# Totals of the cross-attention softmax with queries on the partitions

## The reference

```python
q = (x @ Wq).reshape(B, N, 16, 32).transpose(0, 2, 1, 3)        # 16 heads of 32, N = 224 queries
k = (context @ Wk).reshape(B, M, 16, 32).transpose(0, 2, 1, 3)  # M = 750 keys
v = (context @ Wv).reshape(B, M, 16, 32).transpose(0, 2, 1, 3)
attn = softmax(where(mask, q @ k.T * scale, max_neg), axis=-1)
out = (attn @ v).transpose(0, 2, 1, 3).reshape(B, N, 512) @ Wo
```

## Time and profile before

| | us |
|---|---|
| median of 3 runs | 4072.93 (4070.74 to 4074.32) |
| the profiled execution | 4072.49 |
| its span, from the first to the last instruction | 4070.7 |
| PE busy, whole span | 3752.8 (92%) |
| DVE busy | 2371.8 (58%) |
| ACT busy | 1741.6 (43%) |
| POOL busy | 1300.7 (32%) |

### The profile page before, as it was taken

One profiled execution on the slowest core, in us unless ns is written; L12 is line 12 of the kernel. 1 busy time (PEld: TensorE's weight loads), 2 busy tenths in 40 slices (PEclk: granted clock), 3 DMA queues, 4 the chain that ended last, 5 costly groups with the idle time before them and its releaser, 6 DMA issues. The chain is left out here.

```text
span 4070.7 us, 85297 instructions
## 1 busy us (share of the span) xinstructions
PE 3752.8 (92%) x28101; PEld 3217.9 (79%) x28101; DVE 2371.8 (58%) x5513; ACT 1741.6 (43%) x4280; POOL 1300.7 (32%) x1200
## 2 busy tenths in 40 slices
PE   6999999999679999999999998638999999999997
PEld 5888888888567887778877775637898898988986
DVE  4888888888546665666656664573434433334342
ACT  3545545555335555555555553103333333333332
POOL 1333333333225555555555554001102012022011
PEclk8999999999889999999999998558999999999998
DMA  3122222222233433334333431504333243233231
GB/s 110 50 61 60 56 56 65 52 61 52 91 97 99 108 101 95 103 103 107 101 96 102 103 90 49 148 6 112 94 98 111 76 117 111 80 109 111 85 99 53
DMA packets 319070, 354.23 MB, mean 87 GB/s; under 512 B 45135, under 2 KB 231991, under 8 KB 318996
## 3 DMA queue, kind: packets, MB, share of 16 engines
q1 hardware_dynamic: 309396, 325.67, 29.6%
q0 software_dynamic: 9600, 27.58, 2.4%
HBM read 189.05 MB, written 38.65 MB: 56 GB/s over the span
## 5 line engine op out<-in xcount | busy, mean ns | idle before, releaser
L1482 DVE TENSOR_REDUCE x_mx<-x_psS 112x1 f32<-112x752 f32 x512 | 481.4, 940 | 454.5 <-PE x_psS L1092 450.4
L2200 DVE TENSOR_TENSOR hid<-e_psU,act_g 128x280 f32<-128x280 f32 x256 | 115.1, 450 | 759.1 <-PE e_psU L34 759.1
L1330 ACT ACTIVATE x_pt<-x_psE 125x448 f32<-125x448 f32 x768 | 389.5, 542 | 324.5 <-PE x_psE L1104 318.7
L1004 POOL TENSOR_TENSOR part<-x_pt 125x448 f32<-125x448 f32 x256 | 292.5, 1142 | 608.7 <-ACT x_pt L1330 608.4
L2028 POOL TENSOR_TENSOR ex_y<-ex_y,ex_cur 112x2560 f32<-112x2560 f32 x8 | 45.5, 5691 | 1041.2 <-ACT ex_y L2176 1041.2
L562 POOL TENSOR_TENSOR qks<-qks,cos 128x448 f32<-128x448 f32 x128 | 147.8, 1154 | 699.1 <-DMA qks<-qk 699.1
L1092 PE MATMUL x_psS<-k_st,q_st 97*112 97x376 f32 x1024 | 284.7, 359 | 37.5 <-DVE x_mx L1482 22.9
L2133 ACT ACTIVATE act_g<-e_psG 128x280 f32<-128x280 f32 x256 | 103.6, 405 | 497.6 <-PE e_psG L34 497.5
L32 PE MATMUL e_psG<-ex_hi,g_hi 128*128 128x280 f32 x1024 | 299.6, 293 | 8.0 <-DVE g_lo L2194 6.7
L32 PE MATMUL pj<-xT_hi,win_hi 128*128 128x224 f32 x1024 | 303.1, 296 | 1.8 <-DVE xT_lo L634 1.7
L34 PE MATMUL e_psG<-ex_hi,g_lo 128*128 128x280 f32 x1024 | 298.9, 292 | 0.0
(11 more groups left out here) (280 smaller groups left out, 10847.8 us busy)
## 6 DMA issues: line engine op xcount, KB each, us to landing
k_st<-kT SPq DMA_DIRECT2D x768, 93.8 KB, 2.1
raw_g<-in_L_ffn_wg SPq DMA_DIRECT2D x128, 256.0 KB, 3.2
raw_u<-in_L_ffn_wu SPq DMA_DIRECT2D x128, 256.0 KB, 3.4
raw_d<-in_L_ffn_wd SPq DMA_DIRECT2D x128, 256.0 KB, 2.7
qks<-qk SPq DMA_DIRECT2D x512, 56.0 KB, 2.0
q_st<-qT SPq DMA_DIRECT2D x384, 56.0 KB, 2.0
ctxt<-in_ctx SPq DMA_DIRECT2D x16, 1125.0 KB
xt<-in_x SPq DMA_DIRECT2D x16, 448.0 KB, 3.6
```

Of the source, the lines that this page charges most:

```text
L1004: pool.tensor_tensor(part[:], pt[j][:, 0, :], pt[j][:, 1, :], ALU.add).then_inc(parted, 1)
L1330: act.activation(pt[j][:, i, :], psE[(j + i) % 2][0:KR, 0:2 * T], ACT.Exp, scale=XD ** -0.5).then_inc(exp_done, 1)
L1482: dve.tensor_reduce(mx[:, j, h:h + 1], psS[0:HT, :, 0:376], AX.XY, ALU.max).then_inc(s_taken, 1)
L2200: dve.tensor_tensor(h[i][:, halves[s]], psU[:, 0:CH], act_g[i][:, halves[s]], ALU.mult).then_inc(S["mul"], 1)
```

## The change

The totals are made the other way round. ptsum of a head, 112 queries at a time, becomes the weights, and one column of ones is streamed: 8 products give psTot, 112 queries on the partitions x 8 columns (half h, head j). One reciprocal over 112x8 inverts them. A copy on DVE spreads each column to 32 columns (rzb, 112 x 2 x 128). PE turns both halves back with two transposes into psZ (turn_totals), ACT copies psZ to SBUF (out_totals, rzT, 128x224), and out_y multiplies psY by that. turn_totals stands behind scores (2, 1) on PE; out_totals behind the last exponential of head 2 on ACT; invert is one call, behind maximum (2, 0).

```diff
-            yT, rz = sb(c, "x_yT", [P, KD, T]), sb(c, "x_rz", [P, T])
+            yT, rz, rzb = sb(c, "x_yT", [P, KD, T]), sb(c, "x_rz", [HT, 8]), sb(c, "x_rzb", [HT, 2, P])
+            rzT = sb(c, "x_rzT", [P, T])
...
-            psY, psZ = psYZ[:, 0:T], psYZ[:, T:2 * T]
+            psY, psZ, psTot = psYZ[:, 0:T], psYZ[:, T:2 * T], psYZ[0:HT, 2 * T:2 * T + 8]
...
                         pe.wait_ge(pt_summed, 4 * t + 4)
                         for j in range(4):
-                            m = pe.matmul(psZ[32 * j:32 * j + 32, 0:T], ones[:], ptsum[4 * (g % 2) + j][:], start=True, stop=True)
+                            for h in range(2):
+                                m = pe.matmul(psTot[:, 4 * h + j:4 * h + j + 1], ptsum[4 * (g % 2) + j][:, h * HT:(h + 1) * HT], ones[:, 0:1],
+                                              start=True, stop=True)
                         m.then_inc(z_full, 1)
+
+                    def turn_totals(t):
+
+                        pe.wait_ge(z_spread, t + 1)
+                        for h in range(2):
+                            m = pe.transpose(psZ[:, h * HT:(h + 1) * HT], rzb[:, h, :], ident[0:HT, 0:HT])
+                        m.then_inc(z_turned, 1)
...
                             scores(n, g, 2, 1)
+                            if pprev:
+                                turn_totals(n - 2)
...
                     shifted(n - 1, 3, 3, range(3))
+                    turn_totals(n - 2)
                     values(n - 1, 3)
                     totals(n - 1, 3)
+                    turn_totals(n - 1)
...
+                    def out_totals(t):
+                        act.wait_ge(z_turned, t + 1)
+                        act.activation(rzT[:], psZ, ACT.Copy).then_inc(z_out, 1)
...
                                 exps(n - 1, 2, (2,))
+                            if not (first and g < 2):
+                                out_totals(n - 2)
...
                     for j in range(1, 4):
                         exps(n - 1, j, range(3))
+                    for k in (2, 1):
+                        out_totals(n - k)
...
-                    def invert(t, i):
+                    def invert(t):
 
                         dve.wait_ge(z_full, t + 1)
-                        cols = slice(i * HT, i * HT + HT)
-                        dve.reciprocal(rz[:, cols], psZ[:, cols]).then_inc(recip, 1)
+                        dve.reciprocal(rz[:], psTot).then_inc(recip, 1)
+                        dve.wait_ge(recip, t + 1)
+                        dve.tensor_copy(rzb[:].rearrange("p h (j m) -> p (h j) m", j=4),
+                                        rz[:].unsqueeze(2).to_broadcast((HT, 8, XD))).then_inc(z_spread, 1)
 
                     def out_y(t, g, out=None):
-                        dve.wait_ge(recip, 2 * t + 2)
+                        dve.wait_ge(z_out, t + 1)
...
-                        dve.tensor_tensor(yT[:, g, :], psY, rz[:], ALU.mult).then_inc(y_ready, 1)
+                        dve.tensor_tensor(yT[:, g, :], psY, rzT[:], ALU.mult).then_inc(y_ready, 1)
...
                             if pprev:
-                                invert(n - 2, 0)
+                                invert(n - 2)
                             if g == 2 and not last:
                                 low_ctx(b, 1, 0)
                             maximum(n, 2, 1)
-                            if pprev:
-                                invert(n - 2, 1)
```

More of the change, by code:

```diff
@@ L863, in cross_attention @@
                 sem("x_" + n) for n in ("pj_full", "hi_done", "s_full", "s_taken", "m_high", "valid_done"))
-            st_full, exp_done, y_full, z_full, recip, y_ready, mask_step, parted, pt_summed = (
-                sem("x_" + n) for n in ("st_full", "exp_done", "y_full", "z_full", "recip", "y_ready", "mask_step", "parted", "pt_summed"))
+            st_full, exp_done, y_full, z_full, recip, z_turned, z_spread, z_out, y_ready, mask_step, parted, pt_summed = (
+                sem("x_" + n) for n in ("st_full", "exp_done", "y_full", "z_full", "recip", "z_turned", "z_spread", "z_out", "y_ready", "mask_step", "parted", "pt_summed"))
             pj_free = [sem(f"x_pj_free{i}") for i in range(BANKS)]
@@ L1579, in _ @@
                     for k in (2, 1):
-                        for i in range(2):
-                            invert(n - k, i)
+                        invert(n - k)
                         out_y(n - k, 4 - k)
```

## The result

| kernel | median us | runs | ratio to before, 95% interval |
|---|---|---|---|
| before | 4072.68 | 4070.74 to 4074.32 | |
| changed | 4124.65 | 4122.52 to 4129.37 | 1.0130 (1.0114 to 1.0146) |

The forecast was 4120.5 us in 4092 to 4150, slower: right in sign, and 4 us off in size by the medians (9 us by the profiled execution). The profile shows that this sum came out for partly other reasons. The profiled execution of the changed kernel took 4129.37 us, with a span of 4127.5, 56.8 us longer than before.

A forecast was written before the change was run, and what follows sets the result against it. PE was taken as the bound, busy 1279.2 of 1340 us in the cross-attention loop. The profiled 4072.5 us plus 46 us in the loop and 2 at its end gave 4120.5 us, range 4092 to 4150.

The forecast's parts named there:

- the block of 16 loads: PE's new totals per group: 16 weight loads at 0.098 us, 1.57 us against 0.62 before, +0.95 us.
- g = 1, per group: No wait follows the totals on PE, so block and transposes count in full: 0.95 + 0.24 = 1.19 us.
- g = 2: Block counts whole, 0.95 us, plus 0.4 us because PE waits for the spread copy: 1.35 us.
- end of the stage: Behind the loop, last totals to output projection: 2.70 us becomes 3.4 to 5.1; +2 us taken.
- DVE's relief: DVE loses 1.24 us of work per group, off the path except in g = 2, as PE is the bound.
- The price of a load: PE's load of 112 columns with one column streamed: 0.098 us, near bounds 0.085 and 0.11.
- Rivals 2 and 3: Loads cheap, say 0.05 us each: 4094 us, 9%; or 0.20 us each at the upper clock too: 4223 us, 7%.
- The cover in g = 0 and g = 3: PE's waits behind the totals hide 0.9 us of the block; g = 0 costs 0.29 us, g = 3 0.14.
- The stall that moves in g = 2: PE's 0.92 us wait for the reduce goes; an earlier wait for DVE's spread copy replaces it, +0.4 us.
- The race: In g = 2 DVE's spread copy starts 0.19 us before POOL's first sum, so it isn't locked out.
- Rival 1: In g = 2 the copy loses to POOL and PE waits +1.0 us: 4137 us, 14%.
- The clock: PE's granted clock in the cross-attention loop stays at 0.99, with no cost counted.

The follow-up runs named there:

- The doubled block: Each product of the totals made twice (32 instructions instead of 16): against the changed kernel 4368.81 us; against the kernel with 32 columns streamed 4305.43 us.
- the kernel with the late copy: Kernel with 32 columns streamed, with inversion and spread copy in g = 2 moved behind DVE's second split of the context: 4131.78 us, ratio 1.0149.

## Why the prediction held, step by step

| step | predicted | measured |
|---|---|---|
| the block of 16 loads | 1.57 us | 1.50 us |
| reciprocal and copy | 0.45 us | 0.198 + 0.294 us |
| g = 1, per group | +1.19 us | +1.04 us |
| g = 2 | +1.35 us | +0.99 us |
| g = 3 | +0.14 us | 0.00 us |
| g = 0, at a steady clock | +0.29 us | +0.23 us |
| a batch | +3.0 us | +2.3 us, +3.8 with a fall |
| granted clock | 0.99, no cost | 13 falls, 1.56 us each |
| end of the stage | +2 us | +1.2 us |

The groups are measured from values block to values block, as medians over 13 batches of the loop; g = 0 at a steady clock with 32 columns (+0.23; in the changed kernel's last batch, where the clock did not fall, +0.18).

- **PE is the bound, DVE's relief is worth next to nothing.** Right: putting the load back cost about 4 us in the loop.
- **The price of a load.** Right: 0.098 was taken from the router's spacing at the lower clock level, 0.094 measured. Rivals 2 and 3 fall. The number of weight columns was not varied.
- **The cover in g = 0 and g = 3.** Right, and sharper than thought: the shifted scores start to the hundredth where they did. The doubled block shows that this cover was real and all but used up (g = 3 grew by 1.33 us there).
- **The stall that moves in g = 2.** Right in place and size (1.02 us, 1.1 by experiment). From scores to scores it costs 0.27 us, not 0.4. In each group there is another 0.09 us less: the old totals began 0.47 us behind the transposes of the maxima, the new ones 0.38. I had taken only what came behind their start.
- **The race.** The copy won in all 15 batches that have one, with 0.16 us to spare (1744.77 against 1744.93), where 0.19 was read. Rival 1 fell, but its mechanism was shown twice. That POOL pauses beside the copy in the other groups was wrong: in g = 3 and g = 0 POOL still runs when the copy starts, and by the rows above the copy is spared by hundredths of a us.
- **The clock.** Wrong. I wrote that the clock would stay at 0.99, and it fell in 13 batches: 20 us in the profiled execution, 17 by the medians with and without. The loop without it is 15 x 1.27 + 16 x 0.99 = 35 us, where 46 were predicted. 35 + 20 + 1 = 56, and the spans differ by 56.8. So the forecast holds two errors, -11 and +20 (17 by the medians), that cancel in part. Its closeness is luck to that extent.

The clock was the one cost that I left without a bound. A row that speaks for one was at hand: the router's window, from which I took the price of a load. Its 22.69 us are the matmuls of L1724 alone; all of PE from its first matmul there is this (columns as in the first fence):

```profile
2566.60:2600.00 33.40, 33.38 (x183) 32.93 (x183) 23.75 (x83) 8.92 (x17) 0.00 (x0) 0.50 0.54 166
```

PE is busy without a break from 2566.6 us on, much of it with 8 columns streamed behind such loads, and the clock still stands at 0.50. I took the spacing and did not ask what the clock would mean for a block of the same kind.

## What to carry to other kernels

A matrix product whose work lies in its weights costs by its loads: 16 loads of 112 columns, with one column streamed, take 1.50 us where 8 loads of 32 columns with 224 streamed took about 0.6. Where PE is the bound, moving work from DVE to PE can only pay where a wait goes; look first whether a change of order removes the same wait. And a block of loads that streams little can cost twice: check the granted clock a few microseconds behind it, in many turns of the loop and not in one, since a fall can come in one turn and stay out in the next. If it falls, stream more columns; 32 instead of one were free here, as the loads set the pace (1.51 us for the block against 1.50).

## What the runs showed of the hardware

- PE's clock fell from 2.4 to 1.2 GHz for 3.4 us, 2 us behind a 1.50 us block of loads with one column each, though the records show PE as busy throughout. With 32 columns per load it did not. With a block of 3.0 us it did, 37 times behind the block with one column and 10 times with 32. One fall cost 1.56 us.
- Whether such a block brought a fall depended on when it came: in one kernel always in g = 0, in another in g = 0 or g = 3, with batches between that had none. What decides it stays open.
- Falls began at pauses of PE too: all 7 of the kernel with the late copy, at waits of 2.1 us, and 13 in each doubled kernel, at pauses of 3.3 to 4.4 us.
- A longer loop on PE (64 more matmul instructions in its body than the changed kernel's, each with a load) brought a pause of up to 4.4 us at 13 turns and 119 more packets of instructions.
- A DVE copy of 256 columns took 0.29 us, or 0.98 to 1.05 when a POOL operation of 1.1 us had begun 0.3 us before it. It then ended 0.15 us behind POOL's operation. A copy that began 0.15 us before such an operation ended still took 0.29 us.
